# Nine sequences instead of eight sorted by expert in the first of two top-2 feed-forwards

## Chip, core and metric

The kernel is one program on one core of a Trainium2 chip. The metric is the device time of an execution in microseconds (us), given as the median of some runs. TensorE (PE in the profile; PEld is its weight load) multiplies matrices, VectorE (DVE) and ScalarE (ACT) do element-wise work, GpSimd (POOL) does element-wise work too and issues the indirect transfers (rows scattered or gathered by a list of row numbers), and SyncE (SP) issues the plain ones. Each engine runs its own instructions in order; semaphores order them against each other.

## What is computed

The input is 16 sequences of 512 tokens with 128 features. Three blocks follow each other, each with a residual: a feed-forward of 8 experts with the best two per token, an attention of 16 heads of width 8, and the same feed-forward again. Cut to what matters:

```python
def ffn(x):                               # 8 experts, 128 -> 256 -> 128
    probs = softmax(x @ Wg + bg)
    w, idx = top_k(probs, 2)
    w = w / sum(w)
    comb = sum(one_hot(idx, 8) * w[..., None])
    h = relu(einsum('nd,edh->enh', x, W1) + b1)
    y = einsum('enh,ehd->end', h, W2) + b2
    return einsum('end,ne->nd', y, comb)

def attn(x):                              # per sequence and head
    c = xh - mean_over_tokens(xh)
    return softmax(c @ c.T) @ xh

x = x + 0.5 * ffn(layernorm(x))
x = x + attn(layernorm(x))
x = x + 0.5 * ffn(layernorm(x))
```

## The kernel before, in words

A feed-forward is done in one of two ways. A **whole job** takes one sequence through all 8 experts (`ffn_hidden`, `ffn_expert` on TensorE, 12 multiplications of 512 columns per expert) and weights each expert's output by the gate, which is zero for the six experts not picked. A **sorted** sequence is first *routed*: its normalized rows are ranked by their logits and each row is sent twice, with an indirect transfer, to the regions of its two experts in a buffer in HBM (`sorted_rows`). Later a **tile stream** reads tiles of 512 rows of one expert each, takes each through that expert alone, and writes them to `tile_rows`; the rows are gathered back (`collect`) and added to their sequence (`combine_half`). The number of tiles is fixed: 2 for each sorted sequence and 7 more.

The order in time: the whole jobs of the first feed-forward; attention of the first sequences; the first tile stream; attention of the other sequences; the second tile stream; the whole jobs of the second feed-forward. `NJOBS` is the number of sorted sequences in the first and the second feed-forward (8, 9). `WHOLE` = 16 - 8 = 8 is the number of whole jobs of the first; they take sequences 0 to 7. Attention pauses for the first tile stream after `TILED` = `WHOLE` - 2 sequences.

Everything is ordered by hand. `ffn_tensor`, `ffn_vector`, `ffn_scalar` and `ffn_gpsimd` loop over jobs n and experts e; m = 8n + e. At m TensorE does the first half of expert m + 2 and the second half of expert m, VectorE subtracts for the low half of m + 2 (`halve`, L925) and scales the output of m - 1 (`scale`, L948), ScalarE makes the high half of m + 2 (L1085), GpSimd adds up (`total_up`, L1166).

A **route** of a sorted sequence q stands in pieces between them. `early_tensor`, `early_vector`, `early_scalar`, `early_gpsimd` place the routes that begin in whole jobs; the other routes stand in the attention (`attn_tensor`, `attn_vector`, `attn_gpsimd`). If route q begins in job n, its pieces are:

- job n: statistics on VectorE at e = 2 (L549, L552 on `r_stats`), square root on GpSimd at e = 3, rows scaled on ScalarE at e = 5, turned by TensorE at e = 7 (`route_turn`, L1226), copied by ScalarE;
- job n + 1: logits at e = 0 (`route_logits`, L1233), ranking on VectorE at e = 2, 4, 5 (`route_rank`, L1338 to L1367);
- job n + 2: counting on TensorE at e = 1 (`route_counts`, L1241, L1243), slots and gates on VectorE at e = 2 and 4 (`route_slots`, `route_gates`), the first four of the eight sends on GpSimd at e = 4 to 7 (`send`, L1591), the other four at e = 0 to 3 of job n + 3.

Before, three routes begin in whole jobs (`EARLY` = 3, `early_base(q)` = 1 + 2q: jobs 1, 3, 5) and five in attention, one each beside sequences 0 to 4. A tile of the streams is L1267 to L1304 on TensorE. `clear_tails` (SP, L420) writes zeros behind the last rows of every expert's region once the last route of a group is counted; for the first group that was beside sequence 4 of the attention, for the second beside sequence 14.

Of the kernel before, what the change touches and what calls it, by code (L numbers as in the profile page):

```python
# [15 lines left out]
PAIR = E // CHUNKS  # L16
# [21 lines left out]
NJOBS = 8, 9  # L38
MOST = max(NJOBS)
# [9 lines left out]
XNS = 4  # L49
LOW = -3.0e38  # L50
EARLY = 3
LAST = NJOBS[0] - EARLY - 1, 14
# [119 lines left out]
def rows_slot(q):  # L172

    return q % XNS if q >= 2 else q + 2

# [11 lines left out]
def build(nc, x_in, wg_in, bg_in, w1_rows, b1_in, w2_rows, b2_in, const_in, gates_dram, sorted_rows, tile_rows, out):  # L187
    with ExitStack() as ctx:
# [75 lines left out]
        scratch = sb("scratch", [P, 2 * TILES * E + E * MOST])  # L264
        past = scratch[:, 0:TILES * E].rearrange("p (t e) -> p t e", e=E)
        jump = scratch[:, TILES * E:2 * TILES * E].rearrange("p (t e) -> p t e", e=E)
        over = scratch[:, 2 * TILES * E:2 * TILES * E + E * MOST].rearrange("p (e n) -> p e n", e=E)
        upto = scratch[:, TILES * E:TILES * E + E * E].rearrange("p (e f) -> p e f", e=E)
# [10 lines left out]
        found = sb("found", [P, 2, TOPK, J, D])  # L279
        tile_rows_in = found[:, :, :, :, :].rearrange("p u k j d -> p (u k) (j d)")  # L280
# [21 lines left out]
        W1 = wide[:, 0:E * F].rearrange("p (e f) -> p e f", e=E)  # L302
        W1_last = wide[:, E * F:2 * E * F].rearrange("p (e f) -> p e f", e=E)
        W1s = probs[:, 0:2, :, :].rearrange("p r o t -> p (r o t)").rearrange("p (e f) -> p e f", e=E)
        W2 = probs[:, 2:4, :, :].rearrange("p r o t -> p (r o t)").rearrange("p (e f) -> p e f", e=E)
# [50 lines left out]
        names = """const_in b1_in w1_in_0 w1_in_1 w1_in_2 w1_in_3 w1_last_0 w1_last_1 w1_last_2 w1_last_3 w2_in_0 w2_in_1 w2_in_2 w2_in_3 small_in stored value_set set_up wg_set b2_turned b2_set  # L356
# [14 lines left out]
        x_in_sems = sems("x_loaded", 6)  # L371
# [10 lines left out]
        w1_last = [sm["w1_last_0"], sm["w1_last_1"], sm["w1_last_2"], sm["w1_last_3"]]  # L382
# [28 lines left out]
        def _(sp):  # L411
# [101 lines left out]
            load(2, 2)  # L513
            store_gates(0)
# [1589 lines left out]
```

## Time and profile before

| what | value |
|---|---|
| median of 3 runs | 1068.61 us (1068.46 to 1069.88) |
| the profiled execution's own time | 1070.13 us |
| its span, first to last instruction | 1068.3 us |
| first whole jobs, to the first exponential of the attention | 0 to 221.16 us |
| attention of sequences 0 to 5 | to 402.58 us |
| first tile stream, 23 tiles | to 489.90 us |
| attention of sequences 6 to 15 | to 786.5 us |
| second tile stream, 25 tiles, and second whole jobs | to 1068.3 us |
| busy share of PE / DVE / ACT / POOL | 96% / 77% / 80% / 49% |

The busy shares are means over stages with different limits. In the stages of matrix work TensorE's instructions follow each other with hardly a gap; in the attention ScalarE's do. Lines of the profile are lines of the kernel before; the changed kernel's lines from the middle on are one higher.

### The profile page before, as it was taken

The page shows a single profiled execution, that of the slowest core. Times are in us where ns is not written, and L with a number is a line of the kernel's source. Part 1 is how long each engine was busy: PE and PEld are TensorE (multiplying, and loading weights), DVE is VectorE, ACT ScalarE, POOL GpSimd, SP SyncE. Part 2 cuts the span into 40 slices and gives each one's busy share as a digit, 9 for nine tenths or more (in the row PEclk, how much of TensorE's full clock was granted, in tenths as well). Part 3 has the DMA queues.
Part 4 walks back from the last instruction along what each step waited for, and adds up shares of the span by engine and source line. Part 5 has one row for each costly group of instructions (what it writes and reads, how often), then busy time and mean ns, then how long its engine had stood idle before and what let it go on. Part 6 is the DMA issues. An engine that isn't in the chain of part 4 may idle for free.

```text
span 1068.3 us, 20863 instructions
## 1 busy us (share of the span) xinstructions
PE 1023.2 (96%) x6757; PEld 592.8 (55%) x6757; DVE 826.0 (77%) x2221; ACT 858.2 (80%) x1247; POOL 526.8 (49%) x617
## 2 busy tenths in 40 slices
PE   5899999989999999999999999999999999999996
PEld 3677778842333327884233333333258887777785
DVE  6788888976676667775778877787558767899997
ACT  4555555469999999998999999999999985656563
POOL 4554757554444340003577777674310004777785
PEclk9999999999999999999999999999999999999998
DMA  6443222200000613431011111115124621444342
GB/s 197 141 148 119 93 87 95 86 10 19 19 18 21 176 51 109 146 122 65 29 36 35 37 39 36 38 35 165 44 80 145 220 100 56 162 129 140 140 141 77
DMA packets 57327, 96.23 MB, mean 90 GB/s; under 512 B 8067, under 2 KB 28683, under 8 KB 57219
## 3 DMA queue, kind: packets, MB, share of 16 engines
q1 hardware_dynamic: 47282, 75.77, 21.5%
q0 software_dynamic: 8704, 17.84, 5.5%
q10 hardware_dynamic: 1234, 1.29, 0.4%
q8 instruction: 55, 0.90, 0.4%
q14 instruction: 52, 0.43, 0.1%
HBM read 60.55 MB, written 34.32 MB: 89 GB/s over the span
## 4 chain that ended last, share of the span: by engine, by line
PE 60%; ACT 20%; issue 10%; DVE 4%; POOL 2%; ACTq 0%; DMA 0%; POOLq 0%; DVEq 0%
ACT probs L1879 12%; PE ps L1662 9%; ACT sums L1879 6%; PE ps L1647 4%; PE ps L678 4%; PE ps L694 4%; PE ps L695 4%; PE ps L699 4%; PE ps L680 4%; PE ps L679 4%; PE ps L1281 2%; PE ps L1283 2%; PE ps L1282 2%; PE ps L1292 2%; PE ps L1293 2%
## 5 line engine op out<-in xcount | busy, mean ns | idle before, releaser
L1879 ACT ACTIVATE probs<-ps 128x1024 f32<-128x1024 f32 x342 | 336.2, 1144 | 7.3 <-PE ps L1647 6.0
L1603 POOL DMA_INDIRECT found<-tiles,home x136 | 136.8, 1006 | 224.5 <-ACT sums L1879 112.2
L1085 ACT ACTIVATE high<-ps 128x512 fp32r<-128x512 f32 x240 | 141.4, 596 | 109.8 <-PE ps L680 106.1
L1591 POOL DMA_INDIRECT sorted<-xn,slot x136 | 136.1, 1001 | 134.7 <-ACT probs L1879 85.1
L1662 PE MATMUL ps<-probs,value 128*32 128x512 f32 x1368 | 182.2, 604 | 1.5 <-ACT probs L1879 1.4
L1879 ACT ACTIVATE sums<-ps 128x1024 f32<-128x1024 f32 x170 | 176.9, 1148 | 0.7 <-PE ps L1647 0.2
L925 DVE SCALAR_TENSOR_TENSOR low<-ps,high 128x512 fp32r<-128x512 f32 x240 | 153.5, 681 | 27.2 <-ACT high L1085 26.8
L1166 POOL TENSOR_TENSOR sums<-sums 128x512 f32<-128x512 f32 x89 | 115.6, 1299 | 80.8 <-DVE sums L948 62.0
L1647 PE MATMUL ps<-shared 32*128 32x512 f16 x1024 | 140.8, 384 | 8.6 <-ACT probs L1879 3.0
L1647 PEld LDWEIGHTS ps<-shared 32*128 32x128 f16 x1024 | 38.0, 91 | 136.0 <-ACT probs L1879 74.4
L678 PE MATMUL ps<-xh,weights 128*128 128x512 f32 x240 | 102.6, 427 | 1.7 <-DVE low L925 1.7
L694 PE MATMUL ps<-high,weights 128*128 128x512 f32 x240 | 96.7, 403 | 4.6 <-DVE sums L948 4.6
L695 PE MATMUL ps<-high,weights 128*128 128x512 f32 x240 | 95.8, 399 | 0.0
L680 PE MATMUL ps<-xh,weights 128*128 128x512 f32 x240 | 95.4, 398 | 0.0
L679 PE MATMUL ps<-xl,weights 128*128 128x512 f32 x240 | 95.2, 397 | 0.0
L1662 PE MATMUL ps<-sums,value 128*32 128x512 f32 x680 | 90.6, 604 | 0.3 <-ACT sums L1879 0.2
L699 PE MATMUL ps<-low,weights 128*128 128x512 f32 x240 | 76.0, 399 | 0.0
L1785 DVE COPY shared<-ps 128x1024 f16<-128x1024 f16 x64 | 43.9, 686 | 38.2 <-PE ps L1620 38.2
L1512 DVE SCALAR_TENSOR_TENSOR low<-ps,high 128x512 fp32r<-128x512 f32 x96 | 61.7, 685 | 5.7 <-ACT high L1557 2.3
L1557 ACT ACTIVATE high<-ps 128x512 fp32r<-128x512 f32 x96 | 57.0, 599 | 7.1 <-PE ps L1283 2.5
L1506 DVE TENSOR_TENSOR xl<-ps,xh 128x512 fp32r<-128x512 f32 x48 | 33.1, 690 | 32.6 <-ACT xh L1551 24.2
L1620 PEld LDWEIGHTS ps<-K,wide 128*128 128x128 f16 x512 | 28.9, 97 | 52.4 <-issue 51.6
(190 smaller groups left out, 1911.1 us busy)
## 6 DMA issues: line engine op xcount, KB each, us to landing
wide<-gates SPq DMA_DIRECT2D x32, 512.0 KB, 4.0
probs<-gates SPq DMA_DIRECT2D x28, 512.0 KB, 5.7
found<-sorted SPq DMA_DIRECT2D x48, 256.0 KB, 2.6
tiles<-sums SPq DMA_DIRECT2D x48, 256.0 KB, 2.0
sorted<-zeros SPq DMA_DIRECT2D x16, 512.0 KB
out<-X SPq DMA_DIRECT2D x16, 256.0 KB, 7.8
X<-in_L_attn_x SPq DMA_DIRECT2D x3, 1024.0 KB, 9.5
sorted<-xn,slot POOLq DMA_INDIRECT x136
```

The lines of the kernel that those rows point to most:

```text
L678: nc.tensor.matmul(o, weights[:, e, 0, at], xh[:, u, :], start=True, stop=False)
L679: nc.tensor.matmul(o, weights[:, e, 0, at], xl[:, u, :], start=False, stop=False)
L680: nc.tensor.matmul(o, weights[:, e, 1, at], xh[:, u, :], start=False, stop=True).then_inc(sm["f_hidden"], 1)
L694: nc.tensor.matmul(o, weights[:, e, 2, at], high[:, third(m), c, :], start=(c == 0), stop=False)
L695: nc.tensor.matmul(o, weights[:, e, 3, at], high[:, third(m), c, :], start=False, stop=False)
L925: nc.vector.scalar_tensor_tensor(low[:, third(m), c, :], ps[:, hidden_bank(m, c), :], 0.0, high[:, third(m), c, :].bitcast(F32), ALU.max, ...
L1085: nc.scalar.activation(high[:, third(m), c, :], ps[:, hidden_bank(m, c), :], ACT.Relu).then_inc(sm["f_high"], 1)
L1591: nc.gpsimd.indirect_dma_start(sorted_rows[group_of(q)], bass.IndirectOffsetOnAxis(ap=slot[:, q % XNS, k, j:j + 1], axis=0), xn[:, rows_sl ...
L1603: nc.gpsimd.indirect_dma_start(found[:, q % 2, k, j, :], None, tile_rows[group_of(q)], bass.IndirectOffsetOnAxis(ap=home[:, q, k, j:j + 1] ...
L1647: ins = nc.tensor.matmul(ps[:, score_banks(n).start + odd, :], kq[at, g % 2, 0, j * P:(j + 1) * P], kq[at, g % 2, 1, :], start=True, stop= ...
L1662: ins = nc.tensor.matmul(ps[q * W:(q + 1) * W, MIX, :], value[:, s % 2, sd, j, m, q, :], ring[ring_at(g * UNITS + 2 * j + q // 2)][:, q % ...
L1879: nc.scalar.activation(ring[ring_at(n)], ps[:, score_banks(n), :], ACT.Exp, scale=SCORE).then_inc(sm["a_probs"], 1)
```

## The change

One more sequence is sorted in the first feed-forward: 9 instead of 8. There are 7 whole jobs instead of 8 and 25 tiles in the first stream instead of 23. Five routes begin in whole jobs, one in each of jobs 0 to 4 (`early_base(q)` = q), and four in attention, beside sequences 0 to 3. The first stream comes after 5 sequences of attention. The second group's routes stand beside sequences 5 to 13 instead of 6 to 14.

What goes with it: `xn` has 5 slots instead of 4 and other slot numbers; a small scratch array lies in a part of `found` that the tiles don't use; sequence 7 is loaded early and alone (`load(WHOLE, 1)`), and 4 to 6 without it; TensorE has one more wait (`r_lg`) ahead of `route_counts`; the places of the raw and the shifted weights at the start are exchanged between `wide` and `probs`, since an odd number of whole jobs exchanges the two buffers of spread gates.

```diff
-NJOBS = 8, 9
+NJOBS = 9, 9
...
-XNS = 4
+XNS = 5
 LOW = -3.0e38
-EARLY = 3
-LAST = NJOBS[0] - EARLY - 1, 14
+EARLY = 5
+LAST = NJOBS[0] - EARLY - 1, 13
...
 def early_base(q):
-    return 1 + 2 * q
+    return q
...
 def rows_slot(q):
-    return q % XNS if q >= 2 else q + 2
+    return 2 + q % 3 if q < EARLY else (q - EARLY) % XNS
...
-        scratch = sb("scratch", [P, 2 * TILES * E + E * MOST])
...
         found = sb("found", [P, 2, TOPK, J, D])
+        scratch = found[:, 1, 1, :, :].rearrange("p j d -> p (j d)")
...
-        W1 = wide[:, 0:E * F].rearrange("p (e f) -> p e f", e=E)
-        W1_last = wide[:, E * F:2 * E * F].rearrange("p (e f) -> p e f", e=E)
-        W1s = probs[:, 0:2, :, :].rearrange("p r o t -> p (r o t)").rearrange("p (e f) -> p e f", e=E)
-        W2 = probs[:, 2:4, :, :].rearrange("p r o t -> p (r o t)").rearrange("p (e f) -> p e f", e=E)
+        W1s = wide[:, 0:E * F].rearrange("p (e f) -> p e f", e=E)
+        W2 = wide[:, E * F:2 * E * F].rearrange("p (e f) -> p e f", e=E)
+        W1 = probs[:, 0:2, :, :].rearrange("p r o t -> p (r o t)").rearrange("p (e f) -> p e f", e=E)
+        W1_last = probs[:, 2:4, :, :].rearrange("p r o t -> p (r o t)").rearrange("p (e f) -> p e f", e=E)
...
             load(2, 2)
+            load(WHOLE, 1)
             store_gates(0)
...
                 if n < 4:
-                    load((8, 4, 12)[n - 1], 4)
+                    load(*((8, 4), (4, 3), (12, 4))[n - 1])
...
                 pe.wait_ge(sm["f_lg"], min(n + 2, WHOLE))
+                if early_at(n - 1) is not None:
+                    pe.wait_ge(sm["r_lg"], early_at(n - 1) + 1)
```

Three places in the order of the instructions matter. The first is VectorE at expert 2 of a whole job. Before, in jobs 3 and 5, statistics of one route and slots of an earlier one stand here, and no ranking; `low` is `halve`, `sums` is `scale`, `pos` to `slot` is `route_slots`:

```order
L925 SCALAR_TENSOR_TENSOR low<-ps,high 128x512 x2
L549 BN_STATS r_stats<-X 128x6 x4
L552 BN_AGGR r_moments<-r_stats 128x2 x4
L1374 TENSOR_TENSOR pos<-ps,K 128x32
L1377 TENSOR_TENSOR prod<-pick,pos 128x32 x2
L1380 TENSOR_REDUCE slotf<-prod 128x8
L1382 CAST slot<-slotf 128x8
L948 SCALAR_TENSOR_TENSOR sums<-ps,b2T,probs 128x512
```

In the changed kernel, in jobs 2, 3 and 4:

```order
L926 SCALAR_TENSOR_TENSOR low<-ps,high 128x512 x2
L549 BN_STATS r_stats<-X 128x6 x4
L552 BN_AGGR r_moments<-r_stats 128x2 x4
L1339 TENSOR_REDUCE rtop<-rlg 128x4
L1341 TENSOR_TENSOR alike<-rlg,rtop 128x32
L1343 TENSOR_TENSOR cand<-alike,K 128x32
L1345 TENSOR_REDUCE best<-cand 128x4
L1375 TENSOR_TENSOR pos<-ps,K 128x32
L1378 TENSOR_TENSOR prod<-pick,pos 128x32 x2
L1381 TENSOR_REDUCE slotf<-prod 128x8
L1383 CAST slot<-slotf 128x8
L949 SCALAR_TENSOR_TENSOR sums<-ps,b2T,probs 128x512
```

The first third of the ranking of the route between (`rtop` to `best`) came in; before, it stood in the jobs that had neither statistics nor slots. The second place is TensorE at experts 0 and 1 of a whole job. In the changed kernel's jobs 2 to 4 the logits of one route (L1234) and the counts of the one before it (L1242, L1244) lie one expert apart; before, a job had the one or the other:

```order
L1234 MATMUL ps<-WG,xnT 128x8 x4
L678 MATMUL ps<-xh,weights 128x512
L679 MATMUL ps<-xl,weights 128x512
...
L699 MATMUL ps<-low,weights 128x512 x2
L1242 MATMUL ps<-taken,K 128x32
L1244 MATMUL ps<-taken,ones16 128x32
L1244 MATMUL ps<-taken,ones16 128x24
L1244 MATMUL ps<-taken,ones16 128x16
L1244 MATMUL ps<-taken,ones16 128x8
```

The third is GpSimd at expert 3. Before, a job had at expert 3 the square root of a beginning route or the last send of an earlier one:

```order
L1166 TENSOR_TENSOR sums<-sums 128x512 x2
L583 TENSOR_TENSOR r_vare<-r_moments,K 128x4
L585 TENSOR_TENSOR r_less<-r_moments,K 128x4
L589 TENSOR_TENSOR r_rstd<-r_vare,K 128x4
L592 TENSOR_TENSOR r_offset<-r_less,r_rstd 128x4
L1166 TENSOR_TENSOR sums<-sums 128x512
L1591 DMA sorted_0<-xn,slot 40960x128
```

In the changed kernel's jobs 3 and 4 it has both, and sends stand in all eight experts:

```order
L1167 TENSOR_TENSOR sums<-sums 128x512
L583 TENSOR_TENSOR r_vare<-r_moments,K 128x4
L585 TENSOR_TENSOR r_less<-r_moments,K 128x4
L589 TENSOR_TENSOR r_rstd<-r_vare,K 128x4
L592 TENSOR_TENSOR r_offset<-r_less,r_rstd 128x4
L1592 DMA sorted_0<-xn,slot 40960x128
L1167 TENSOR_TENSOR sums<-sums 128x512
L1592 DMA sorted_0<-xn,slot 40960x128
```

## Rows read from the trace of the kernel before

**Rows 1.** The page: busy time of three engines over the span

```profile
PE 1023.2 (96%) x6757; PEld 592.8 (55%) x6757; DVE 826.0 (77%) x2221; ACT 858.2 (80%) x1247; POOL 526.8 (49%) x617
```

**Rows 2.** Busy time per stretch: 20 tiles, then jobs between two `ffn_back`

```profile
core 0: us, PE busy (x) PEld busy (x) DVE busy (x) ACT busy (x) POOL busy (x), PEclk, DMA share, GB/s
413.29:486.39 73.10, 73.01 (x397) 61.34 (x396) 54.53 (x86) 65.53 (x99) 0.00 (x0) 1.00 0.38 131
110.44:136.08 25.64, 25.64 (x131) 20.56 (x130) 22.50 (x62) 15.23 (x32) 19.95 (x24) 1.00 0.30 100
136.08:160.62 24.54, 24.54 (x124) 19.33 (x123) 21.93 (x57) 13.24 (x27) 13.90 (x16) 1.00 0.26 92
186.25:209.91 23.66, 23.66 (x112) 19.03 (x111) 22.41 (x48) 10.26 (x18) 13.35 (x13) 1.00 0.30 97
```

**Rows 3.** Timeline of PE: start, us, what, its idle time before

```profile
124.98 0.40 PE L694 MATMUL ps<-high,weights 128*128 128x512 f32 x1
...
128.21 0.40 PE L694 MATMUL ps<-high,weights 128*128 128x512 f32 x1
...
131.89 0.39 PE L694 MATMUL ps<-high,weights 128*128 128x512 f32 x1
...
134.68 0.39 PE L694 MATMUL ps<-high,weights 128*128 128x512 f32 x1
```

**Rows 4.** Timeline of PE: first and last `back` of the 20 tiles

```profile
413.29 0.60 PE L1304 MATMUL ps<-K,sums 128*128 128x128 f32 x4
...
486.39 0.60 PE L1304 MATMUL ps<-K,sums 128*128 128x128 f32 x4
```

**Rows 5.** Busy time per stretch: attention of sequences 3 and 14

```profile
313.42:343.12 29.70, 29.14 (x255) 9.41 (x255) 21.01 (x75) 29.57 (x34) 12.65 (x17) 1.00 0.06 19
727.24:756.94 29.70, 29.27 (x256) 9.53 (x256) 20.88 (x72) 29.57 (x35) 10.91 (x13) 1.00 0.56 161
```

**Rows 6.** Timeline of DVE in job 3, experts 2 and 6

```profile
111.10 0.86 DVE L549 BATCH_NORM_STATS2 r_stats<-X 128x6 f32<-128x128 f32 x4
...
112.16 0.16 DVE L1374 TENSOR_TENSOR pos<-ps,K 128x32 f32<-128x32 f32 x1
...
113.05 0.75 DVE L948 SCALAR_TENSOR_TENSOR sums<-ps,b2T,probs 128x512 f32<-128x512 f32 x1
...
123.10 1.29 DVE L925 SCALAR_TENSOR_TENSOR low<-ps,high 128x512 fp32r<-128x512 f32 x2 [1.72 <-ACT high L1085]
```

**Rows 7.** Stretches cut at VectorE's starts: statistics and slots, gates, ranking 1 to 3

```profile
111.10:113.05 1.95, 1.95 (x10) 1.58 (x9) 1.85 (x14) 1.18 (x2) 0.25 (x1) 1.00 0.00 0
118.22:118.78 0.56, 0.56 (x4) 0.44 (x4) 0.49 (x6) 0.49 (x1) 0.50 (x1) 1.00 1.03 227
136.44:137.25 0.81, 0.81 (x7) 0.68 (x5) 0.71 (x6) 0.00 (x0) 0.64 (x2) 1.00 0.00 0
143.85:144.69 0.84, 0.84 (x5) 0.67 (x4) 0.74 (x6) 0.74 (x2) 0.00 (x0) 1.00 0.83 210
146.55:147.70 1.15, 1.15 (x6) 0.93 (x5) 1.01 (x6) 0.49 (x2) 0.26 (x1) 1.00 1.01 381
```

**Rows 8.** Timeline of POOL in job 3, and the page's group of all sends

```profile
118.28 1.19 POOL L1591 DMA_INDIRECT sorted<-xn,slot  x1 [0.19 <-POOL sums L1166]
...
L1591 POOL DMA_INDIRECT sorted<-xn,slot x136 | 136.1, 1001 | 134.7 <-ACT probs L1879 85.1
```

**Rows 9.** Job 0: PE's longest wait, and clock and busy time behind it

```profile
31.28 0.73 PE L694 MATMUL ps<-high,weights 128*128 128x512 f32 x1 [2.63 <-DVE sums L948]
...
31.28:35.15 3.87, 3.87 (x11) 3.01 (x11) 2.33 (x5) 0.20 (x1) 0.03 (x1) 0.56 0.00 0
```

**Rows 10.** Sequences 13 and 14: last gather, first combine after it, zeros written

```profile
720.80 0.97 POOL L1603 DMA_INDIRECT found<-tiles,home  x1 [0.30 <-issue]
...
725.70 2.30 DVE L1476 SCALAR_TENSOR_TENSOR X<-found,gates_sorted,X 128x128 f32<-128x128 f32 x8
...
732.12 13.61 SPq L420 DMA_DIRECT2D sorted<-zeros  x8
```

More of the change, by code:

```diff
@@ L263, in build @@
         ends = sb("ends", [P, E])
-        scratch = sb("scratch", [P, 2 * TILES * E + E * MOST])
[L265 to L268, printed above, removed]
         skip = sb("skip", [P, E])
@@ L279, in build @@
         found = sb("found", [P, 2, TOPK, J, D])
+        scratch = found[:, 1, 1, :, :].rearrange("p j d -> p (j d)")
+        past = scratch[:, 0:TILES * E].rearrange("p (t e) -> p t e", e=E)
+        jump = scratch[:, TILES * E:2 * TILES * E].rearrange("p (t e) -> p t e", e=E)
+        over = scratch[:, 2 * TILES * E:2 * TILES * E + E * MOST].rearrange("p (e n) -> p e n", e=E)
+        upto = scratch[:, TILES * E:TILES * E + E * E].rearrange("p (e f) -> p e f", e=E)
         tile_rows_in = found[:, :, :, :, :].rearrange("p u k j d -> p (u k) (j d)")
@@ L354, in build @@
         count_ps = ps[:, MISC, 128:128 + E]
-        names = """const_in b1_in w1_in_0 w1_in_1 w1_in_2 w1_in_3 w1_last_0 w1_last_1 w1_last_2 w1_last_3 w2_in_0 w2_in_1 w2_in_2 w2_in_3 small_in stored value_set set_up wg_set b2_turned b2_set
+        names = """const_in b1_in w1_in_0 w1_in_1 w1_in_2 w1_in_3 w2_in_0 w2_in_1 w2_in_2 w2_in_3 small_in stored value_set set_up wg_set b2_turned b2_set
  w1_shifted w1_high w1_low w2_high w2_low
@@ L370, in build @@
         sm = {n: sem(n) for n in names}
-        x_in_sems = sems("x_loaded", 6)
+        x_in_sems = sems("x_loaded", 7)
         tail_cleared = sems("tail_cleared", 2)
@@ L381, in build @@
         w1_in = [sm["w1_in_0"], sm["w1_in_1"], sm["w1_in_2"], sm["w1_in_3"]]
-        w1_last = [sm["w1_last_0"], sm["w1_last_1"], sm["w1_last_2"], sm["w1_last_3"]]
         w2_in = [sm["w2_in_0"], sm["w2_in_1"], sm["w2_in_2"], sm["w2_in_3"]]
@@ L394, in x_loaded @@
         def x_loaded(s):
-            return x_in_sems[s if s < 2 else 2 + s // 4]
+            return x_in_sems[{0: 0, 1: 1, 2: 2, 3: 2, 4: 3, 5: 3, 6: 3, 7: 4}.get(s, 3 + s // 4)]
         def stream(a, b):
@@ L490, in load_last @@
                 at = slice(q * PAIR, (q + 1) * PAIR)
-                sp.dma_start(W1_last[:, at, :], w1_rows.rearrange("e d f -> d e f")[P - 1:P, at].to_broadcast([P, PAIR, F])).then_inc(w1_last[q], 16)
+                sp.dma_start(W1_last[:, at, :], w1_rows.rearrange("e d f -> d e f")[P - 1:P, at].to_broadcast([P, PAIR, F])).then_inc(w1_in[q], 16)
             def load_w2(q):
@@ L819, in shift_w1 @@
         def shift_w1(dve, q):
-            dve.wait_ge(w1_in[q], 16)
-            dve.wait_ge(w1_last[q], 16)
+            dve.wait_ge(w1_in[q], 2 * 16)
             nc.vector.tensor_tensor(pair(W1s, q)[0:P - 1], pair(W1, q)[0:P - 1], pair(W1_last, q)[0:P - 1],
```

## The prediction, made before the changed kernel was run

> **What bounds the kernel now.** I read the page first. TensorE (PE) is busy 96% of the span, ScalarE 80%, VectorE 77%, GpSimd 49% [rows 1]. These are means over stages, so next I cut the time into stretches. In a whole job of the first feed-forward PE is busy for the entire stretch: 25.64 of 25.64 us, 24.54 of 24.54, 23.66 of 23.66; VectorE is next with 22.50, 21.93 and 22.41 [rows 2]. The first tile stream is the same case: 73.01 of 73.10 us busy for 20 tiles [rows 2, 4]. The attention is bound elsewhere: of the 29.70 us of a sequence ScalarE is busy for 29.57, and PE's 29.1 to 29.3 there are matmuls that wait in its pipeline for the exponentials; sequences 3 and 14 both take 29.70 us [rows 5]. So a whole job, a route beside it and a tile each cost what PE spends on them, and a route beside the attention costs nothing as long as ScalarE goes on.
>
> **The whole job removed.** I need the price of a plain job, without any route. A job's stretch runs from one `ffn_back` to the next, that is from expert 2 to expert 2. The one of 25.64 us holds a route's turn and logits, the one of 24.54 us a route's counts [rows 2]. The plain distance of two experts is 134.68 - 131.89 = 2.79 us; with the turn between it is 128.21 - 124.98 = 3.23, with the logits 131.89 - 128.21 = 3.68 [rows 3]. So the turn costs 0.44 and the logits 0.89, together 1.33 us, a plain job 25.64 - 1.33 = 24.31 us, and the counts 24.54 - 24.31 = 0.23. **One whole job less: -24.31 us.** Its loads, stores and gate transfers go with it; none of them ended a wait of PE in these stretches.
>
> **Two more routes beside whole jobs.** On PE each costs 1.33 + 0.23 = 1.56 us: **+3.12 us**. The piece in job 0 (turn of route 0) stands in its last expert. Taken away is one route beside the attention; its price there is nothing, since sequences 3 and 14 carry a route and ScalarE is full [rows 5]. A sequence without a route could be shorter by a few tenths, and only if ScalarE had room; the bound is the 29.70 - 29.57 = 0.13 us that it is not busy. I take 0.
>
> **Two more tiles.** From the first to the last `back` of 20 tiles 486.39 - 413.29 = 73.10 us pass, 3.655 per tile [rows 4]. **+7.31 us.** Their weights, loads and stores lie beside the matmuls, as they do for the 20; ScalarE is the next engine there with 65.53 of 73.10 [rows 2].
>
> **Does the cover hold?** In jobs 2, 3 and 4 every piece of a route meets the others. PE then needs 24.31 + 1.56 = 25.87 us per job. VectorE: the job of 25.64 us held statistics, slots (111.10 to 113.05, 1.95 us) and gates (0.56), busy 22.50 [rows 2, 6, 7]. What comes on top is the ranking of the route between, 0.81 + 0.84 + 1.15 = 2.80 us [rows 7]: 25.30 us. By the other stretch (ranking inside, busy 21.93) it is 21.93 + 1.95 + 0.56 = 24.44 us. Both lie under 25.87, by 0.6 to 1.4 us: VectorE just keeps up. How late it may be for a moment is a different question. At expert 2 it has 1.95 us of extra work now and 2.76 us after. Behind it wait `scale` and `halve` of the next expert, and for these PE's `ffn_hidden` and `ffn_expert` two experts on. After the 1.95 us VectorE had caught up so far that it waited 1.72 us for ScalarE at expert 6 of that job [rows 6], while PE never waited. The 0.81 us more at expert 2, 0.84 at 4 and 1.15 at 5 eat this pause (and smaller ones) and leave it about 1 us late at the worst, with low halves wanted one expert, 2.79 us, or more behind their making. I take 0 for PE's waits. Without the cover each us that VectorE needs over 25.87 costs one us per full job.
>
> GpSimd: the job of 25.64 us had 19.95 us of work with six sends [rows 2]; two more at 1.00 us [rows 8] make 22, and 8 x 0.17 us between a sum and its send 23.3 of 25.87. It keeps up, 2.5 us spare. The last send of a slot is issued at expert 3 and its slot is written again by ScalarE at expert 5, two experts (some 6 us) on.
>
> Job 5 (the last but one) carries ranking, slots and gates beside the first preparation of the attention; before, that job had 22.41 us of VectorE's work in 23.66 and no slots or gates [rows 2]. Slots (113.05 - 112.16 = 0.89) and gates (0.56) make 23.86 [rows 6, 7] against PE's 23.66, which stays (one route's counts before and after). Here VectorE exceeds PE by 0.2 us; it may end 0.2 to 1 us later, and the next job, which is as before, takes it up. I take 0; the bound is +0.5.
>
> **The rest.** The new wait for `r_lg` at expert 1 asks for a copy of 0.2 us that ScalarE does one expert earlier. Sequence 7's 256 KB stand in SP's queue ahead of the first gates' store, which waits for ScalarE anyway; at the worst they move it by 1 us. Exchanging `wide` and `probs`, the fifth slot of `xn` and the scratch in `found` add no instruction and no wait.
>
> **The sum**, against the profiled execution: -24.31 + 3.12 + 7.31 = **-13.88 us**. Its own time is 1070.13, its span 1068.3 us: after, 1056.25 and a span of 1054.4. The median of the runs shown, 1068.61, lies 1.52 us under the profiled execution, so the median after is 1068.61 - 13.88 = **1054.7 us**.
>
> **The rivals.**
>
> *VectorE becomes the bound in the full jobs* (0.24). For: 25.3 of 25.87 us is 98%, and busy time leaves out what passes between two dependent small instructions: the three parts of the ranking show 0.71 + 0.74 + 1.01 = 2.46 us busy in 2.80 us [rows 7]. Counted by its pauses instead, with the one of 1.72 us [rows 6] as the only one, it needs at the most 25.64 - 1.72 + 2.80 = 26.72 us, 0.85 over; smaller pauses bring this down. Against: it starts each job with a pause to eat. At 0.3 to 1 us over in jobs 2 to 4, and as much in job 5, the cost is 1 to 3.5 us: 1055.7 to 1058.2.
>
> *The first two jobs* (0.05). In job 0 PE waits 2.63 us for VectorE, and over the next 3.87 us its granted clock is 0.56, hence mostly at 1.2 GHz [rows 9]. Route 0's statistics (1.06 us, 112.16 - 111.10 [rows 6]) stand in VectorE's order behind this wait and in front of the gating of job 1. If they reach PE they cost 1.06 us and once more such a slow stretch, 3.87 x 0.44 = 1.7 us: 1057.5. Against: they come in a place where VectorE next waits for ScalarE.
>
> *Gathers behind the zeros* (0.04). Zeros are written by SP for 13.61 us in sequence 14, DMA share 0.56 [rows 5, 10]. This moves to sequence 13, where there are now gathers for the last sorted sequence, which there were not. If they land late VectorE waits at the combine, and ScalarE behind it. Before, 4.9 us lie between the last gather's issue and the combine [rows 10]. The zeros begin 732.12 - 727.24 = 4.9 us into the sequence and their issues end at 18.5; sequence 13 began one period before sequence 14, at 727.24 - 29.70 = 697.54, and its last gather 23.3 us into it. It would have to take over 4.9 us; I price it at 1 to 3 us: 1055.7 to 1057.7.
>
> *Slower: the sends hold GpSimd up* (0.03). The 32 sends of routes 0 to 3 stand beside a VectorE that hardly pauses. If each took longer, `total_up` comes late, then `scale`, then PE. Spare are 2.5 us per job. To use up the gain of 13.88 us in four jobs' worth of sends takes (13.88/4 + 2.5)/8 = 0.75 us per send, 1.75 us instead of 1.00; beyond that the kernel is slower. With 2 us each it is 1054.7 + 4 x (8 - 2.5) = 1076.7. Against: beside a VectorE busy 88% of the time sends took 1.19 us at the most of those shown, 1.00 in the mean of all 136 [rows 8]. The Trainium skill (SBUF — State Buffer, section "SBUF: two separate sides") has a rule for this mechanism: a DMA issued by GpSimd needs a port that VectorE can lock, and one of about 620 ns took about 3100 ns beside a VectorE copy. By its figures, an estimate, eight sends would cost 20 us more per job and the kernel would be some 70 us slower; the rows show no such send, and that is why it has so small a chance.
>
> **How the numbers follow.** The forecast has 0.64, the rivals 0.24, 0.05, 0.04 and 0.03. The predicted time is 1054.7. The lower end allows for 0.13 us per sequence in a few sequences and for half a us of error in each of three terms: 1053.2. The upper end takes in nearly all of the first rival and the second and third: 1058.0. About 0.2% (2.1 us) is what a measurement of this kernel can tell from no change; all cases but the last are faster by more. Faster 0.95, same 0.02, slower 0.03.
>
> **What would show it.** Right: jobs 2 to 4 of the changed kernel are 25.9 us from `ffn_back` to `ffn_back` with PE busy throughout; VectorE's pauses there all but vanish; 24 tile distances of 3.655 us; 29.70 us for each sequence; the second feed-forward unchanged. Wrong: PE waiting for VectorE's `low` or `sums` from job 2 on (the first rival, then its clock is to be looked at as well), for `gate` or `sums` in jobs 0 and 1, VectorE waiting for `found` in sequence 13, sends over 1.2 us.

## The result, and the profile after

The changed kernel takes 1062.2 us (median of 6 runs, 1061.58 to 1063.49), the kernel before 1069.1 in the 6 runs beside it; ratio 0.9938, 95% interval 0.9925 to 0.9951. It is faster, by 6.9 us where 13.9 were forecast, and 1062.2 lies above the range. The profiled execution took 1062.25 us with a span of 1060.2; forecast for it were 1056.25 and 1054.4. So 6.0 us have to be found in the trace. The other 1.5 us between forecast and median come from the step from profile to median: before, the profiled execution lay 1.5 us above its median, after it lies on it.

The busy times between two `ffn_back`, for the six intervals (core, then sum and mean left out):

```profile
core 0: us, PE busy (x) PEld busy (x) DVE busy (x) ACT busy (x) POOL busy (x), PEclk, DMA share, GB/s
60.80:86.66 25.86, 25.86 (x136) 20.58 (x135) 23.53 (x66) 15.33 (x33) 13.84 (x18) 1.00 0.34 113
86.66:112.52 25.86, 25.86 (x136) 20.58 (x135) 24.63 (x75) 15.33 (x33) 19.57 (x24) 1.00 0.42 139
112.52:139.77 27.25, 26.22 (x136) 20.34 (x135) 25.25 (x74) 15.22 (x33) 20.54 (x24) 1.00 0.28 97
139.77:167.52 27.75, 26.48 (x136) 20.27 (x135) 26.61 (x75) 15.21 (x33) 21.40 (x25) 1.00 0.29 96
167.52:192.32 24.80, 24.24 (x113) 18.76 (x112) 23.27 (x55) 10.27 (x18) 19.25 (x18) 1.00 0.30 108
192.32:210.06 17.74, 15.12 (x80) 9.98 (x78) 16.80 (x47) 5.76 (x9) 12.38 (x15) 1.00 0.03 8
```

I call them intervals 1 to 6. The first two are what was forecast, 25.86 with PE busy throughout. The granted clock (PEclk) is 1.00 in all six, so the clock plays no part in what follows. 3, 4, 5 and 6 were to be 25.87, 25.87, 23.66 and 15.86 (the last as before); they are longer by 1.4, 1.9, 1.1 and 1.9 us, together 6.3, and PE pauses in each. Interval 2 holds six sends, 3 and 4 hold eight: the last two sends of the route before, at experts 2 and 3, come in. PE's and ScalarE's instructions are the same in 2 and 3. The rest of the span:

```profile
367.86:448.69 80.83, 80.75 (x437) 67.51 (x436) 59.93 (x94) 72.34 (x109) 0.00 (x0) 1.00 0.38 131
297.71:327.40 29.69, 29.25 (x256) 9.48 (x255) 20.22 (x69) 29.56 (x34) 10.92 (x13) 1.00 0.56 161
689.54:719.23 29.69, 29.26 (x256) 9.49 (x255) 22.43 (x79) 29.56 (x34) 18.56 (x21) 1.00 0.61 176
```

22 tiles take 80.83 us, 7.73 more than the 20 of [rows 4], where 7.31 were forecast. Attention sequences 3 and 13 take 29.69 as before [rows 5]; 13 is the one in which gathers and zeros now meet. So the attention holds, the tiles cost 0.4 us more than said, and nearly all that is missing lies between 112 and 210 us. What the engines wait for between 60.8 and 210.06 us (engine, line, what it waited for: total, times, longest; main rows on PE, on transfers and on the key rows):

```profile
ACT xn L574 <- DMA sorted<-xn,slot: 5.6, 2, 3.1
...
PEld ps L694 <- DVE sums L949: 3.7, 8, 1.0
...
PE ps L1227 <- DVE xl L855: 1.7, 2, 1.0
...
PE ps L694 <- DVE sums L949: 1.2, 2, 0.6
...
DVE wide L1762 <- POOL wide L1889: 1.0, 1, 1.0
```

PE waits for VectorE (`sums`, `xl`), as the first rival has it. But two rows there are not VectorE's doing: ScalarE waits twice for sends of a slot that it is to write again, and VectorE waits for GpSimd's clearing of `wide` (the key rows of the attention). The timeline of job 3 at experts 3 and 4, GpSimd (POOL) and then VectorE (DVE), and one row of job 4, show a third thing:

```profile
117.91 1.04 POOL L589 TENSOR_TENSOR r_rstd<-r_vare,K 128x4 f32<-128x4 f32 x1
119.03 0.20 POOL L592 TENSOR_TENSOR r_offset<-r_less,r_rstd 128x4 f32<-128x4 f32 x1
119.39 1.03 POOL L1592 DMA_INDIRECT sorted<-xn,slot  x1 [0.16 <-issue]
120.45 1.30 POOL L1167 TENSOR_TENSOR sums<-sums 128x512 f32<-128x512 f32 x1
...
120.29 1.52 DVE L1348 TENSOR_TENSOR pick<-K,best 128x32 f32<-128x32 f32 x1
121.85 0.19 DVE L1350 SCALAR_TENSOR_TENSOR rest<-pick,rlg 128x32 f32<-128x32 f32 x1
...
147.89 2.04 DVE L1348 TENSOR_TENSOR pick<-K,best 128x32 f32<-128x32 f32 x1
```

`pick` is an operation of 0.19 us. Here it takes 1.52 and, one job on, 2.04 us, and it ends at 121.81, when GpSimd's addition (120.45 + 1.30 = 121.75) has ended. In front of that addition stand, on GpSimd, the four steps for `r_rstd` and a send: at expert 3 of jobs 3 and 4 they now meet, in the kernel before they never did (routes in jobs 1, 3 and 5 only, so no route's last four sends fell in a job with an `r_rstd`).

A smaller hold of this kind was there in the kernel before. In its job 3 `below`, 0.19 us where nothing holds it, took 0.54, while GpSimd ended a send (128.16) and began `square`:

```profile
127.76 0.54 DVE L866 TENSOR_TENSOR below<-lg,top 128x32 f32<-128x32 f32 x1
...
128.19 0.74 POOL L1153 TENSOR_TENSOR square<-cent,K 128x256 f32<-128x256 f32 x1
```

### The profile page after: what moved, and what is told of

The parts are those of the page before. It is cut to its first block, busy times and chain, and to the rows that moved or that the text cites. A ratio compares the mean times of both kernels' runs of the same rounds, so it can differ in the third digit from the quotient of the medians.

```text
span 1060.2 us, 20742 instructions
## 1 busy us (share of the span) xinstructions
PE 1009.6 (95%) x6697; PEld 578.3 (55%) x6697; DVE 820.5 (77%) x2219; ACT 855.8 (81%) x1244; POOL 531.8 (50%) x624
## 4 chain that ended last, share of the span: by engine, by line
PE 53%; ACT 19%; issue 11%; DVE 9%; POOL 3%; DMA 1%; ACTq 0%; POOLq 0%; DVEq 0%
ACT probs L1880 12%; PE ps L1663 9%; ACT sums L1880 6%; PE ps L1648 4%; PE ps L678 3%; PE ps L694 3%; DVE low L926 3%; PE ps L699 3%; PE ps L695 3%; PE ps L680 3%; PE ps L679 3%; PE ps L1282 2%; PE ps L1284 2%; PE ps L1283 2%; PE ps L1293 2%
## 5 line engine op out<-in xcount | busy, mean ns | idle before, releaser
L1604 POOL DMA_INDIRECT found<-tiles,home x144 | 144.9, 1007 | 236.5 <-ACT sums L1880 120.2
L1086 ACT ACTIVATE high<-ps 128x512 fp32r<-128x512 f32 x224 | 131.4, 595 | 96.5 <-PE ps L680 93.2
L1592 POOL DMA_INDIRECT sorted<-xn,slot x144 | 144.7, 1005 | 110.1 <-ACT probs L1880 67.2
L926 DVE SCALAR_TENSOR_TENSOR low<-ps,high 128x512 fp32r<-128x512 f32 x224 | 143.1, 681 | 17.3 <-ACT high L1086 17.1
L1167 POOL TENSOR_TENSOR sums<-sums 128x512 f32<-128x512 f32 x82 | 106.6, 1300 | 59.0 <-DVE sums L949 40.4
L678 PE MATMUL ps<-xh,weights 128*128 128x512 f32 x224 | 96.0, 428 | 2.8 <-DVE low L926 2.8
L694 PE MATMUL ps<-high,weights 128*128 128x512 f32 x224 | 90.4, 404 | 5.8 <-DVE sums L949 5.8
L680 PE MATMUL ps<-xh,weights 128*128 128x512 f32 x224 | 89.0, 397 | 0.0
L679 PE MATMUL ps<-xl,weights 128*128 128x512 f32 x224 | 88.9, 397 | 0.0
L695 PE MATMUL ps<-high,weights 128*128 128x512 f32 x224 | 88.8, 396 | 0.0
L699 PE MATMUL ps<-low,weights 128*128 128x512 f32 x224 | 70.9, 398 | 0.0
L1513 DVE SCALAR_TENSOR_TENSOR low<-ps,high 128x512 fp32r<-128x512 f32 x100 | 64.3, 684 | 6.0 <-ACT high L1558 2.3
L1558 ACT ACTIVATE high<-ps 128x512 fp32r<-128x512 f32 x100 | 59.4, 599 | 7.0 <-PE ps L1284 2.7
L1546 ACT ACTIVATE chosen<-weights 128x1024 fp32r x50 | 52.8, 1059 | 8.1 <-issue 7.3
```

The source lines that it names most:

```text
L678: nc.tensor.matmul(o, weights[:, e, 0, at], xh[:, u, :], start=True, stop=False)
L679: nc.tensor.matmul(o, weights[:, e, 0, at], xl[:, u, :], start=False, stop=False)
L680: nc.tensor.matmul(o, weights[:, e, 1, at], xh[:, u, :], start=False, stop=True).then_inc(sm["f_hidden"], 1)
L694: nc.tensor.matmul(o, weights[:, e, 2, at], high[:, third(m), c, :], start=(c == 0), stop=False)
L695: nc.tensor.matmul(o, weights[:, e, 3, at], high[:, third(m), c, :], start=False, stop=False)
L926: nc.vector.scalar_tensor_tensor(low[:, third(m), c, :], ps[:, hidden_bank(m, c), :], 0.0, high[:, third(m), c, :].bitcast(F32), ALU.max, ...
```

## The experiments

Two theories stood at the start, the third came up with the first two runs. **A, slots:** routes 3 and 4 write `xn` slots whose last send (expert 3) took 6.2 us to land, and ScalarE's wait at expert 5 explains the loss. **B, load:** VectorE is full by its own instructions (the first rival). **C, GpSimd's crowding:** the sends make GpSimd late, and its late operations hold up single VectorE operations and the clearing of the key rows. The runs lie on several chips; the ratio compares each with the kernel before on the same chip.

**Rows of routes 3 and 4 in another buffer.** Theory A alone.

```
 def rows_slot(q):
-    return 2 + q % 3 if q < EARLY else (q - EARLY) % XNS
+    return XNS + q - 3 if 3 <= q < EARLY else 2 + q if q < EARLY else (q - EARLY) % XNS
...
+        def rows_of(q):
+            return xn[:, rows_slot(q), :, :] if rows_slot(q) < XNS else found[:, 0, rows_slot(q) - XNS, :, :]
```

Expected: 

> The changed kernel with one difference: the rows of routes 3 and 4 lie in a free part of found instead of the slots of routes 0 and 1, so that ScalarE's scaling of their rows waits for no send. Theory A (slot reuse): in the changed kernel ScalarE waited 2.56 and 3.1 us for the last send of routes 0 and 1 in jobs 3 and 4, and everything late in jobs 3 to 6 follows from it; without it the stretches between two ffn_back go from 27.25, 27.75, 24.80 and 17.74 us to 25.9, 25.9, 23.7 and 15.9, and the time falls by 5 to 6 us. Theory B (VectorE is full): the stretches with a full route lose only what ScalarE waited, PE goes on waiting for VectorE's sums in jobs 5 and 6, the stretches of 24.80 and 17.74 us stay within 0.5 us, and the time falls by 2 to 3.5 us.

Measured: 1061.4 us (ratio to before 0.9926, 0.9912 to 0.9940). ScalarE's wait is gone. Intervals 25.86, 25.86, 26.34, 26.85, 24.84, 17.75: 3 and 4 are 0.9 us shorter each, 5 and 6 not at all. Taking the slot wait away gives 1.8 of the 6.3 us in the intervals and about 1 us in the time, where A expected 5 to 6 and B 2 to 3.5. A falls as the whole cause; the intervals 5 and 6 stayed as B had said.

**Eight sends in four experts.** More crowding on GpSimd, no wait for a slot: the eight sends of a route stand two by two at experts 4 to 7.

```
-                send(pool, early_at(n - 2), e - 4)
-            if n < WHOLE and early_at(n - 3) is not None and e < 4:
-                send(pool, early_at(n - 3), e + 4)
+                send(pool, early_at(n - 2), 2 * (e - 4))
+                send(pool, early_at(n - 2), 2 * (e - 4) + 1)
```

Expected: 

> The changed kernel with one difference: the eight sends of an early route all stand at experts 4 to 7 of job n + 2, two per expert, instead of one each at experts 4 to 7 and 0 to 3 of the next job. The slot is then free half a job earlier. Theory A: the wait of ScalarE is gone and the time falls by about as much as with the rows in found, less what GpSimd's sums come late behind two sends (0 to 2 us). Theory B (VectorE full, and held up by GpSimd's lock): GpSimd is late at experts 4 to 7 in jobs 2 to 5, VectorE waits for its sums, and little is won: 0 to 2 us.

Measured: 1065.5 us (0.9965, 0.9952 to 0.9978), some 3 us slower than the changed kernel where both theories had expected a gain or no change, intervals 25.86, 25.86, 26.96, 27.45, 26.27, 18.84. ScalarE's wait for sends is gone here too. VectorE's instructions are the same; only their company on GpSimd is not. Its trace shows where the time went: `cent`, 0.41 us elsewhere, takes 2.2 us in each of jobs 2, 3 and 4, from inside a send to behind the addition that follows it. In job 3:

```profile
132.13 0.96 POOL L1591 DMA_INDIRECT sorted<-xn,slot  x1 [0.30 <-issue]
133.12 1.29 POOL L1166 TENSOR_TENSOR sums<-sums 128x512 f32<-128x512 f32 x1
...
132.51 2.19 DVE L863 TENSOR_TENSOR cent<-lg 128x256 f32<-128x256 f32 x1
```

This speaks for C.

**No early sends.** On the kernel with rows in `found`; GpSimd's calls are dropped, and eight plain transfers fill the sorted rows with zeros instead. It leaves out the rows of the first four sorted sequences.

```
-            if n < WHOLE - 1 and early_at(n - 2) is not None and e >= 4:
-                send(pool, early_at(n - 2), e - 4)
-            if n < WHOLE and early_at(n - 3) is not None and e < 4:
-                send(pool, early_at(n - 3), e + 4)
```

Expected: 

> The kernel of the run with rows in found (rows of routes 3 and 4 in the buffer found), without the 32 sends of routes 0 to 3 in the whole jobs; this leaves out part of the computation: the rows of the first four sorted sequences are never placed, the sorted buffer's first 1280 rows of each expert are filled with zeros by eight plain transfers in jobs 4 to 6 instead, so the first group's feed-forward runs on zeros for them. Theory B (VectorE is full in jobs 3 to 6 by its own instructions: 25.3 us of 25.87): the intervals between one whole job's transposes back and the next stay 25.86, 25.86, 26.34, 26.85, 24.84, 17.75 within 0.2 us, and the time stays at 1061.4. Theory C (GpSimd comes late behind its sends, its additions then run beside VectorE's small operations on two SBUF inputs and hold them for 1.3 to 1.7 us each, and the clearing of the key rows in the last job comes late): the stretches at VectorE's pick and rest (0.19 us instead of 1.52 and 1.90) vanish, intervals 3 and 4 go to 25.86 and 25.9, intervals 5 and 6 to 24.0 and 16.0, attention starts some 3.5 to 4 us earlier than 204.14, and the time is 1057 to 1058. A mix (intervals 3 and 4 as in C, 5 still 24.8) gives 1059.

Measured: 1056.05 us (0.9874, 0.9859 to 0.9890). Its windows:

```profile
61.35:87.21 25.86, 25.86 (x136) 20.58 (x135) 23.55 (x66) 15.34 (x33) 13.87 (x18) 1.00 0.32 113
87.21:113.07 25.86, 25.86 (x136) 20.57 (x135) 24.51 (x75) 15.35 (x33) 13.65 (x18) 1.00 0.36 124
113.07:138.94 25.87, 25.87 (x136) 20.58 (x135) 24.52 (x75) 15.34 (x33) 13.64 (x18) 1.00 0.52 158
138.94:164.81 25.87, 25.87 (x136) 20.58 (x135) 24.31 (x75) 15.34 (x33) 13.20 (x16) 1.00 0.47 159
164.81:188.60 23.79, 23.79 (x113) 18.91 (x112) 23.27 (x57) 10.27 (x18) 11.23 (x11) 1.00 0.47 145
188.60:204.46 15.86, 14.65 (x80) 10.03 (x78) 14.65 (x44) 5.76 (x9) 9.59 (x11) 1.00 0.01 2
```

These are the forecast's intervals to 0.13 us, with every route piece in place on PE, ScalarE and VectorE. VectorE is busy for 24.3 to 24.5 of 25.87 us, which is the lower of the prediction's two sums (24.44) and not 25.30; in interval 3 it is 0.7 us less than in the changed kernel. `pick` takes 0.20 us. The attention starts at 199.84 us, where the forecast's own sum puts it (221.16 before, less 24.31, plus 3.12: 199.97). B falls as the main cause: VectorE's own load fits. The sends, or what they make late, are what costs.

**No send at expert 3.** The last four sends at experts 0, 1, 1, 2 (rows in `found`).

```
-            if n < WHOLE and early_at(n - 3) is not None and e < 4:
-                send(pool, early_at(n - 3), e + 4)
+            if n < WHOLE and early_at(n - 3) is not None and e < 3:
+                for i in ((4,), (5, 6), (7,))[e]:
+                    send(pool, early_at(n - 3), i)
```

Expected: 

> The kernel of the run with rows in found, and the last four sends of each early route stand at experts 0, 1, 1 and 2 of the job instead of 0, 1, 2 and 3, so that none stands beside GpSimd's steps for r_rstd at expert 3. Theory C: GpSimd's addition at expert 3 starts 1.0 us sooner and has ended before VectorE's pick; pick takes 0.2 us instead of 1.52, interval 3 falls from 26.34 to 25.9 and interval 4 from 26.85 to 26.0; intervals 5 and 6 hold (24.8, 17.7), since the last job still has its sends; time 1060.0. Theory B: a send's place does not matter, intervals as before within 0.2 us, time 1061.4.

Measured: 1059.4 us (0.9910, 0.9896 to 0.9923), intervals 25.86, 25.86, 25.87, 25.87, 25.16, 17.74. The same 32 sends; in each job the last two stand one expert (3 us) earlier, and intervals 3 and 4 are whole again. `pick` in job 3 takes 0.41 us. Interval 5 grew by 0.3: two sends now stand beside `a_rstd` at expert 1 of job 5, and VectorE's `alike` there takes 1.18 us instead of 0.19.

**None in the last whole job.** As above, and route 3's last four sends in the odd units of the first attention sequence.

```
-            if n < WHOLE and early_at(n - 3) is not None and e < 3:
+            if n < WHOLE and early_at(n - 3) is not None and e < 3 and n < WHOLE - 1:
...
+                if s == 0 and i in (1, 3, 5, 7):
+                    pool.wait_ge(sm["a_probs"], first + PACE[i])
+                    send(pool, early_at(WHOLE - 4), 4 + i // 2)
```

Expected: 

> As the run before, and the last four sends of route 3 stand in the first attention sequence's odd units instead of the last whole job, so that GpSimd clears the key rows as early as in the kernel before. Theory C: VectorE's casts of wide wait for nothing and take 0.69 us each (1.00 us waited and 1.84 us before), interval 6 falls from 17.75 to 15.9 or 16.3, attention starts 1.5 to 2 us earlier; time 1058.3. Theory B: interval 6 stays above 17.2, because VectorE has fallen behind in job 5; time 1060 to 1061.

Measured: 1058.1 us (0.9898, 0.9883 to 0.9913), intervals as in the run before but 25.05 and 15.94 at the end. Interval 6 drops by 1.8 us. What stood there in the changed kernel, GpSimd and then VectorE:

```profile
187.96 0.98 POOL L1592 DMA_INDIRECT sorted<-xn,slot  x1 [0.17 <-issue]
188.95 0.96 POOL L1887 MEMSET wide<- 128x1024 f16 x1
189.97 0.39 POOL L1889 MEMSET wide<- 128x64 f16 x1
190.28 1.00 POOL L1592 DMA_INDIRECT sorted<-xn,slot  x1
191.30 1.05 POOL L1895 TENSOR_TENSOR square<-cent 128x512 f32<-128x512 f32 x1
...
190.46 0.69 DVE L1762 CAST wide<-cent 128x1024 f16<-128x1024 f32 x1 [1.02 <-POOL wide L1889]
191.07 1.84 DVE L1763 CAST wide<-cent 128x1024 f16<-128x1024 f32 x1
```

The key rows are cleared behind a send, VectorE waits 1.02 us for that, and its second cast takes 1.84 us (0.69 in the kernel before). It ends at 192.91, 0.56 us after GpSimd's send and square (192.35), so most of the cast came when they were done.

**Job 5 too.** In job 5 the two sends beside `a_rstd` at expert 1 go to expert 2, and the one at expert 2 to expert 3.

```
-            if n < WHOLE and early_at(n - 3) is not None and e < 3 and n < WHOLE - 1:
-                for i in ((4,), (5, 6), (7,))[e]:
+            if n < WHOLE and early_at(n - 3) is not None and e < 4 and n < WHOLE - 1:
+                for i in (((4,), (5, 6), (7,), ()), ((4,), (), (5, 6), (7,)))[n == WHOLE - 2][e]:
```

Expected: 

> The kernel with no send at expert 3 and none in the last job, and in whole job 5 the two sends that stood beside GpSimd's steps for a_rstd at expert 1 moved to experts 2 and 3 (one at 0, two at 2, one at 3). If GpSimd's late addition beside VectorE's alike (1.17 us instead of 0.19) makes interval 5 long, it falls from 25.05 to 23.8 to 24.1, which is VectorE's own count or PE's; time 1057.0. If VectorE's own load makes it long, it stays at 24.9 to 25.1; time 1058.1.

Measured: 1057.4 us (0.9883, 0.9867 to 0.9900), interval 5 24.19 (23.8 to 24.1 expected), attention start 199.85 us, the same as without any send. This is the kernel that beats both: 12.2 us under the one before, against 6.9 for the changed kernel, each in its own comparison.

**Only the sends moved.** The changed kernel with its own slots, sends placed as in the run before.

```
-            if n < WHOLE and early_at(n - 3) is not None and e < 4:
-                send(pool, early_at(n - 3), e + 4)
+            if n < WHOLE - 1 and early_at(n - 3) is not None and e < 4:
+                for i in (((4,), (5, 6), (7,), ()), ((4,), (), (5, 6), (7,)))[n == WHOLE - 2][e]:
+                    send(pool, early_at(n - 3), i)
...
+                if s == 0 and i in (1, 3, 5, 7):
+                    pool.wait_ge(sm["a_probs"], first + PACE[i])
+                    send(pool, early_at(WHOLE - 4), 4 + i // 2)
```

Expected: 

> The changed kernel with its own row slots (routes 3 and 4 still in the slots of routes 0 and 1), and only the early sends placed as in the kernel that had job 5 put right too: last four at experts 0, 1, 1, 2 (in job 5 at 0, 2, 2, 3), and those of route 3 in the first attention sequence. Routes 0 and 1 now have sent their last row block one expert (3 us) sooner, so ScalarE's wait at expert 5 of jobs 3 and 4 (2.6 and 3.1 us in the changed kernel) goes to 0 or 0.3 us. If GpSimd's place and lateness explain the loss, intervals are 25.86 to 25.9 four times, then 24.2 and 15.9, and the time is within 0.5 us of 1057.4. If the slots cost in their own right, 3 and 4 are above 26.2 and the time is 1058.2 or more.

> The changed kernel itself on the same chip as the run beside it: 1062.2 within 0.6 us, intervals 3 to 6 27.3, 27.8, 24.8, 17.7.

Measured: 1066.4 us and, for the changed kernel beside it, 1072.0; before 1075.0 (ratios 0.9913, 0.9899 to 0.9927, and 0.9970, 0.9957 to 0.9984). The expected times were missed by 9 and 10 us, the intervals were not: 25.86 four times, 24.26, 15.96 with the sends moved, and 25.86, 25.86, 27.01, 27.80, 24.80, 17.78 without. On this chip the attention sequences 6 to 13 took 30.1 to 32.0 us in both traces instead of 29.70, 13 the longest with 31.7 and 32.0; why stays open, and a trace of the kernel before on it was not taken. So there the rival of the gathers behind the zeros is not excluded. Side by side, moving the sends is worth 5.6 us, and in the whole jobs the slots cost nothing any more (no wait of ScalarE for a send is left): the wait for them was a result of where the last send stood. The first attention sequence took 33.8 us in this trace against 32.9 in those of the changed kernel and of job 5; what held it is open, and the slots are not ruled out there.

**One more power in place of a send.** The kernel without early sends, and a GpSimd power on 128x4 where the send at expert 3 stood.

```
                 norm_pool(pool, "r_", early_at(n), early_at(n) % 2)
+                if n >= 3:
+                    nc.gpsimd.tensor_tensor(filler[:, n - 3, :], vare["r_"][:, early_at(n) % 2, :], each(MINUS_HALF), ALU.pow)
```

Expected: 

> The kernel without the early sends (which leaves out the rows of the first four sorted sequences), and in whole jobs 3 and 4 one more GpSimd power on 128x4 (1.02 to 1.07 us, as its own step for r_rstd) stands right behind r_offset at expert 3, where the send stood. No transfer is issued there. If it is GpSimd's lateness of 1 us that costs (its addition then starts at about 120.7 instead of 119.70, beside VectorE's pick), pick or rest takes 1.3 to 1.7 us instead of 0.2, interval 3 rises from 25.87 to 26.1 or 26.4 and interval 4 from 25.87 to 26.2 or 26.9, attention starts 0.5 to 1.5 us later than 199.84, and the time is 1056.6 to 1057.5. If it is the send itself (its descriptors or its transfer), all intervals stay at 25.87 and the time at 1056.05.

Measured: 1057.95 us (0.9886, 0.9869 to 0.9902; without the power 0.9874, so the two are not apart by their times). Intervals 25.83, 25.83, 25.83, 25.87, 24.53, 15.87. The expected rise of 3 and 4 did not come, but interval 5 rose by 0.7 us and the attention started at 200.69, 0.85 us later (0.5 to 1.5 expected; 0.2 of it stands in the first job). The hold of 1.0 us in job 3 fitted into VectorE's slack; after the one of 0.8 us in job 4 VectorE began interval 5 late (`rtop` 1.0 us after the interval's start instead of 0.2), and there it has the least room. The hold itself came without a send near it (GpSimd, VectorE in job 3, VectorE in job 4; there GpSimd's addition ran from 147.42 to 148.73):

```profile
119.83 1.01 POOL L767 TENSOR_TENSOR filler<-r_vare,K 128x4 f32<-128x4 f32 x1
120.80 1.30 POOL L1177 TENSOR_TENSOR sums<-sums 128x512 f32<-128x512 f32 x1
...
120.99 1.17 DVE L1358 TENSOR_TENSOR pick<-K,best 128x32 f32<-128x32 f32 x1
...
147.61 0.19 DVE L1362 TENSOR_REDUCE after<-rest 128x4 f32<-128x32 f32 x1
147.84 0.92 DVE L1364 TENSOR_TENSOR diff<-after,rtop 128x4 f32<-128x4 f32 x1
```

`pick` ends at 122.16, the addition at 122.10. In job 4 the reduction, with one input, takes its usual 0.19 us inside the addition, and `diff`, with two inputs in SBUF, takes 0.92 instead of 0.16 and ends with it. So a late addition holds VectorE without any send; that it also costs PE is shown in interval 5 only.

**Gates later, alone and with all moves.** VectorE's four gate steps of the five early routes (0.56 us each time, 0.79 where `den` is held) are taken out of jobs 2 to 6 and done once in the attention's second unit; first on the kernel with rows in `found`, then on that of job 5.

```
-                if e == (7 if n == WHOLE - 1 else 4):
-                    route_gates(dve, early_at(n - 2))
...
+                if g == 1:
+                    route_gates(dve, 0, EARLY)
```

Expected: 

> The kernel of the run with rows in found, and VectorE's four small steps for the gates of a route (0.93 us for each of five early routes) are taken out of the whole jobs and done for all five at once in the second unit of the first attention sequence; sends unchanged. It takes 0.93 us off VectorE in jobs 2 to 6 and moves nothing on GpSimd. Theory B (VectorE full): VectorE catches up 0.9 us more in each job, interval 4 falls from 26.85 to 26.0, interval 5 from 24.84 to 23.9, interval 6 from 17.75 to 17.2; time 1059. Theory C alone (single operations held up by GpSimd, 1.3 us each): interval 3 still 26.3, 4 26.4; interval 5 24.4; time 1060.5.

> The kernel of the run before, and VectorE's gate steps of the five early routes done together in the first attention sequence (0.93 us less for VectorE in each of jobs 2 to 6). With the stretched operations gone, PE is the bound in jobs 1 to 4 and nothing more is to be had there: intervals 25.86 four times, 23.7 to 23.8, 15.86; at most 0.2 us better than the run before, 1056.8 to 1057.0. If VectorE's load still bound anything by itself, interval 5 falls by 0.1 to 0.9 us below that of the run before.

Measured: alone 1059.85 us (0.9914, 0.9900 to 0.9927), intervals 25.84, 25.83, 25.88, 26.51, 24.09, 17.75; with all moves 1057.46 (0.9882, 0.9865 to 0.9898), 25.84, 25.83, 25.83, 25.83, 23.69, 15.86. In the first, VectorE still has a `pick` of 1.85 and a `rest` of 1.89 us, but with up to 0.8 us more room per job PE feels them less (1.5 us in all). That lies between what B (1059) and C alone (1060.5) expected: it takes the holds and the load together. In the second the time is that of the run without this edit: once the long holds are gone (`pick` in job 3 still takes 0.58 us), VectorE's load is worth 0.5 us in interval 5, too little to tell in the medians (in the profile a first job that ended 1.2 us later covers it).

## Why the prediction was wrong

- **The sum's terms on PE were right.** A job less, routes at 1.56 us: intervals 1 and 2 at 25.86, and the attention's start at 199.84 and 199.85 us where nothing disturbs, against 199.97 by the sum.
- **The step that failed is "Does the cover hold? ... I take 0 for PE's waits".** It was 5.5 us at the attention's start (205.44): 6.3 us in intervals 3 to 6, less 0.8 by which the first job ran ahead of the sum. I had added up busy times whose durations came from rows where none was held: beside the part of the ranking with `pick` GpSimd is busy for 0.00 us [rows 7]. GpSimd's part was checked by its sum alone (23.3 of 25.87 us; 20.5 and 21.4 busy were measured in intervals 3 and 4, so it does keep up), not by what falls together at one expert: four steps of `r_rstd` (1.7 us), a send and an addition at expert 3 of jobs 3 and 4.
- **The first rival has the right place and the wrong reason.** PE did wait for VectorE, by more than its 1 to 3.5 us. But without the sends the same VectorE work fits. Its load, 24.3 to 24.5 us measured without the sends, is what makes a held operation reach PE; it is no bound by itself. The runs split the 6.3 us so: 1.8 for the slot wait, 1.5 for the send at expert 3, 1.8 for the sends in the last job (moved away 0.1 is left); in interval 5 the changed kernel's 1.1 end at 0.5 once its sends are placed well. The first two are not independent: moving the sends does away with both. Half a us of interval 5 is VectorE's load (it goes when the gates go too).
- **The slot sentence ("two experts (some 6 us) on") had both times wrong.** From the start of route 0's last send (119.39) to the point at which ScalarE was ready to write the slot again (125.61 less 2.56 of waiting: 123.05) it was 3.7 us, not 6. And I had counted a send as done with its 1.00 us on GpSimd, while this one had landed only 6.2 us after its start. That is not a send's usual time: the page gives a median of 2.3 us from issue to landing for all 144. In these 6.2 us the DMA engines were 95% busy, with transfers of 512 KB of the spread gates; in the 6.3 us before them, 5% (the two stretches from send to send, DMA share and GB/s last):

```profile
113.13:119.39 6.26, 6.26 (x33) 4.98 (x32) 5.54 (x22) 4.21 (x9) 3.88 (x7) 1.00 0.05 13
119.39:125.61 6.22, 6.22 (x36) 4.52 (x34) 6.01 (x16) 2.63 (x6) 4.65 (x5) 1.00 0.95 337
```

  One expert earlier, in the run with only the sends moved, ScalarE waits for no send. That the gates' transfers are what kept it was not tested by a run.
- **"The next job, which is as before, takes it up" was false.** The last whole job was not as before: it had sends, ahead of the clearing of the key rows, and cost 1.9 us instead of giving back.
- **The rule of the Trainium skill was applied in one direction only.** I read SBUF — State Buffer, "SBUF: two separate sides", as VectorE holding GpSimd's sends. The same section says that whichever starts first has the pair for the whole instruction, and names VectorE operations with two SBUF inputs. The traces agree with that direction beside GpSimd's additions: `pick`, `diff` and `rest` end with the addition (0.03 to 0.06 us behind it), the reduction between them does not wait. Beside a send they agree only in part (last section). The section also names VectorE's two-port modes; whether `den` (below) ran in one, no run shows. The other direction, the one that the prediction had priced, does not show: sends took 1.005 us in the mean of 144.
- **Tiles** 7.7 us instead of 7.31: two of the distances are 3.87 and 3.88 us instead of 3.655. Why is open.
- **Gathers behind the zeros** (sequence 13 at 29.69 in the profile of the changed kernel; on the chip where it took 31.7 it is not excluded) and **the first two jobs** did not come true.
- **From profile to median** 1.5 us were carried over from three runs and one profile; more runs of before gave 1069.0 to 1069.6 as its median (1075.0 on the chip of the last pair).

## What to carry to other kernels

When work is added to a helper engine, don't stop at its sum per stage: write down what stands together at one step, and look at which small operations of the nearly full engine fall beside it. Here VectorE, busy for 94% of a job, took one hold of 1.0 us without PE noticing; the next one, of 0.8 us, came out as 0.7 us where the load was 98% (23.3 of 23.8 us). And the time from a transfer's issue to its landing belongs to the life of its buffer, read from the moment in question and not from a mean (2.3 us in the median here, 6.2 us where it counted): give a send its place by when the buffer is wanted, or move it into a stage where the engine has nothing else to do.

## What the runs showed of the hardware

Beside a GpSimd addition of 1.30 us, small VectorE operations with two SBUF inputs did not end before it: they took 0.3 us when they began near its end and 1.17 (`pick`) or 0.92 us (`diff`) when they began 0.2 or 0.4 us after its start, instead of 0.16 to 0.19. A send by itself mostly did not hold them, but a few that began 0.36 us or more into a send with an addition right behind it were held until the addition had ended: `pick` 2.04 us, `rest` 1.90, the larger `cent` (128x256) 2.2. Even a VectorE operation on 128x4 with one input was held to the end of a send, right after two with two inputs had gone through:

```profile
121.92 0.98 POOL L1592 DMA_INDIRECT sorted<-xn,slot  x1 [0.17 <-POOL sums L1167]
...
122.30 0.16 DVE L1354 TENSOR_TENSOR diff<-after,rtop 128x4 f32<-128x4 f32 x1
122.38 0.18 DVE L1355 TENSOR_TENSOR alike<-rest,after 128x32 f32<-128x32 f32 x1
122.48 0.40 DVE L1389 TENSOR_SCALAR den<-second 128x4 f32<-128x4 f32 x1
```

These are rows of the changed kernel: `den` takes 0.16 us where nothing holds it, and here it ends at 122.88 with the send (122.90). It was held beside an addition too (206.59 to 207.16, addition to 207.14). Which part of a send holds VectorE, no run shows. VectorE's large operations that read PSUM kept their 0.74 and 0.68 us throughout.
